# Moving first inputs, square roots and constant products across stage borders in an eleven-stage audio tower

## The reference, cut to what matters

```python
h = tokenizer(x)                       # conv1 + max over 8, conv2 + max over 4, self attention, conv3
h = h + attention0(layernorm(h))       # its own norm1, local and linear attention, then norm2 and a GELU MLP of 256
h = h + experts0(layernorm(h))         # 16 experts of 128, top 2 of a softmax gate, layernorm at the end
h = h + attention1(layernorm(h))       # 8 heads over 128 tokens, softmax
h = h + experts1(layernorm(h))         # 32 experts of 16, the best one alone, ReLU

def layernorm(x): return (x - mean(x)) / sqrt(var(x) + 1e-5)
```

## Time and profile before

| | us |
|---|---|
| median of 3 executions | 1010.16 |
| lowest and highest | 1009.18, 1010.31 |
| the profiled execution's own time | 1008.98 |
| its span, first to last instruction | 1007.1 |

### The profile page before, as it was taken

The page is one execution under the profiler, slowest core; times in us unless marked ns, Lnnn a source line. Parts: engine busy times, 40 slices in busy tenths (PEclk is TensorE's granted clock), DMA queues, the critical chain, the costliest instruction groups (busy, mean ns, idle before and its releaser), DMA issues. The chain is left out here.

```text
span 1007.1 us, 35503 instructions
## 1 busy us (share of the span) xinstructions
PE 937.3 (93%) x12674; PEld 676.7 (67%) x12674; DVE 704.2 (70%) x1964; ACT 642.4 (64%) x1204; POOL 520.2 (52%) x814
## 2 busy tenths in 40 slices
PE   7799987799889899999999997899999999969998
PEld 2345555577657688888888884566666666648887
DVE  3667744577758468787887876788888888865443
ACT  1245465687766568777777865777777777734444
POOL 0000114688675477878787876356565656452110
PEclk7799998899989899999999998999999999989999
DMA  8633000000000000000000000000000000000001
GB/s 224 146 43 59 5 2 1 2 0 0 1 2 0 3 3 4 0 0 0 0 0 0 1 2 2 1 2 1 0 0 0 0 0 0 1 2 18 21 21 28
DMA packets 10769, 14.89 MB, mean 15 GB/s; under 512 B 9296, under 2 KB 9424, under 8 KB 9680
## 3 DMA queue, kind: packets, MB, share of 16 engines
q1 hardware_dynamic: 10608, 13.63, 6.2%
q10 hardware_dynamic: 96, 0.39, 0.2%
HBM read 11.92 MB, written 2.10 MB: 14 GB/s over the span
## 5 line engine op out<-in xcount | busy, mean ns | idle before, releaser
L1771 ACT ACTIVATE e_hid<-ps,cst 128x512 f32<-128x512 f32 x256 | 155.3, 688 | 55.4 <-PE ps L1546 55.4
L1484 POOL TENSOR_TENSOR e_acc<-e_acc,e_part 128x512 f32<-128x512 f32 x96 | 122.4, 1275 | 33.7 <-DVE e_part L1702 26.8
L1558 PEld LDWEIGHTS ps<-ew,e_hid 128*64 128x64 f32 x4096 | 124.8, 138 | 22.0 <-issue 10.4
L1558 PE MATMUL ps<-ew,e_hid 128*64 128x64 f32 x4096 | 133.8, 224 | 0.0
L1546 PE MATMUL ps<-e_xs,ew 64*128 64x256 f32 x1024 | 129.8, 393 | 0.0
L1702 DVE TENSOR_TENSOR e_part<-ps,e_wt 128x512 f32<-128x512 f32 x128 | 86.8, 687 | 45.1 <-PE ps L1558 37.9
L1546 PEld LDWEIGHTS ps<-e_xs,ew 64*128 64x128 f32 x1024 | 94.9, 189 | 15.3 <-issue 3.0
L1965 POOL TENSOR_TENSOR a_sum<-a_part 128x256 f32<-128x256 f32 x64 | 46.7, 729 | 94.7 <-DVE a_part L2071 94.7
L2033 PEld LDWEIGHTS ps<-cst,a_ex 128*128 128x128 f32 x512 | 55.8, 141 | 51.5 <-issue 51.5
L2060 DVE TENSOR_REDUCE a_rmax<-ps 128x8 f32<-128x1024 f32 x64 | 78.1, 1221 | 15.9 <-PE ps L2025 14.1
L2025 PE MATMUL ps<-a_u,a_xs 64*128 64x512 f32 x256 | 71.9, 638 | 12.7 <-DVE a_diff L2063 11.6
(11 more groups left out here) (258 smaller groups left out, 2014.7 us busy)
## 6 DMA issues: line engine op xcount, KB each, us to landing
x_in<-x_dram SPq DMA_DIRECT2D x45, 128.0 KB, 5.0
cst<-cst_dram SPq DMA_DIRECT2D x1, 3101.0 KB, 13.5
out_dram<-e_res SPq DMA_DIRECT2D x16, 128.0 KB, 2.0
ew<-ew_dram SPq DMA_DIRECT2D x1, 1024.0 KB, 15.5
cst<-cst_dram SPq DMA_DIRECT2D x1, 704.0 KB, 4.5
ew<-ew_dram SPq DMA_DIRECT2D x1, 512.0 KB, 16.7
x_in<-x_dram ACTq DMA_DIRECT2D x3, 128.0 KB, 6.0
cst<-cst_dram SPq DMA_DIRECT2D x1, 153.5 KB, 4.3
```

Of the source, the lines that this page charges most:

```text
L1484: eng.tensor_tensor(acc[:, :, :, :], acc[:, :, :, :], part[n % RING][:, :, :, :], ALU.add).then_inc(sum_sb.sem, 1)
L1558: mm = eng.matmul(m.ps[rows, 6 + n % 2, to:to + C], hid[e % 8][:, a:a + C], w2[:, e * C:e * C + C], start=True, stop=True)
L1771: nc.scalar.activation(hid[e % 8][:, :].rearrange("p (r t) -> p r t", r=2), m.ps[:, 2 + 2 * (n % 2):4 + 2 * (n % 2), j * 256:(j + 1) * 256 ...
```

## The change

It moves work across stage borders and adds no arithmetic. In its parts:

1. **Start.** Each of the first six DMAs is split in two halves of 64 KB. The first halves count on a new semaphore `x_first`. `conv1` of round 0 waits for them before its first quarter, and for the second halves before its third. SP waits for the first halves alone.
2. **End of the tokenizer.** The bias products, which used bank 6, use bank 0 and stand in round 8 on PE, with their copies on DVE. `weights(2)` goes to round 8 as well, `weights(3)` to the head of round 9, before `attend`. The first turn of a0 stands before the last `conv3`. ACT copies a0's first inputs before `scaled()`, and no longer loads the Exp table there.
3. **First rounds of a0.** DVE does the late variance and inverse of n1 before round 0. The late square root stands on ACT right after the first `features`, then the Exp table is loaded once.
4. **a0 to m0.** PE turns m0's first inputs before the last `attend` and `out`; ACT copies them before `attended`; DVE does the inverse before the last `context`.
5. **m0 to e0.** The square root of n3 and a reload of the GELU table stand on ACT at the head of m0's round 15; its inverse at the end of that round on DVE. PE turns e0's first inputs before the last `out`. ACT copies them before the Exp table is loaded. The bias transposes of e0's round 0 move into the round. The hidden banks change places (4, 5 for even pairs, 2, 3 for odd).
6. **e0 to a1.** POOL makes the inputs of a1's round 1 after e0's last `fold` and `scale`. DVE does `result(14)` and `count(14)` after a1's first scores.
7. **a1 to e1.** The square root of n6 stands after sample 0 of a1's last round, its inverse after sample 1. POOL makes e1's inputs of rounds 0 and 1 after its samples 2 and 3 of that round. PE turns and ACT copies the first ones before a1's last samples, and the first routing (`logits`, then `choose` on DVE) stands among them.

```diff
-    def load_half(eng, g, b, r):
+    def load_half(eng, g, b, r, some=slice(0, H2), sem=None):
         for k in range(3):
-            rows = m.x[bass.ds(g * GS, GS), :, r * H2 + k:r * H2 + k + H2].rearrange("s c l -> (s c) l")
+            lo = r * H2 + k + some.start
+            rows = m.x[bass.ds(g * GS, GS), :, lo:lo + some.stop - some.start].rearrange("s c l -> (s c) l")
             a = 64 * r + 16 * k
-            eng.dma_start(x_in[b][a:a + 16, :], rows).then_inc(x_sem[b], 16)
-
-    m.load_first = lambda eng: load_half(eng, 0, 0, 1)
+            eng.dma_start(x_in[b][a:a + 16, some], rows).then_inc(sem or x_sem[b], 16)
+
+    def load_first(eng, r):
+
+        load_half(eng, 0, 0, r, slice(0, H2 // 2), x_first)
+        load_half(eng, 0, 0, r, slice(H2 // 2, H2))
+
+    m.load_first = lambda eng: load_first(eng, 1)
 
     def sp(eng):
 
-        load_half(eng, 0, 0, 0)
-        eng.wait_ge(x_sem[0], 96)
+        load_first(eng, 0)
+        eng.wait_ge(x_first, 96)
...
-            if h == 0:
+            if isinstance(g, int) and g == 0 and h == 0:
+                eng.wait_ge(x_first, 96)
+            elif h == (2 if isinstance(g, int) and g == 0 else 0):
                 eng.wait_ge(x_sem[b], (g - b) * 48 + 96)
...
+            last = not among(g, 0, NG)
+            tail = not among(g, 0, NG - 1) and not last
+            if last:
+                weights(3)
             if among(g, 2, NG + 1):
                 attend(g - 2, b)
             if among(g, 1, NG - 2):
                 conv1(g + 1, 1 - b, 3)
-            if not among(g, 0, NG - 1):
-                weights(2 * (g - NG))
-            if not among(g, 0, NG):
-                weights(3)
-                m.early["a0_pe"](eng)
+            if tail:
+                weights(0)
+                m.early["a0_biases"](eng)
+            if last:
+                m.early["a0_turn"](eng)
             if among(g, 2, NG + 1):
                 conv3(g - 2)
-            if not among(g, 0, NG - 1) and among(g, 0, NG):
+            if tail:
                 weights(1)
+                weights(2)
...
                 m.early["a0_scaled"](eng)
+                m.early["a0_biases_sb"](eng)
...
+                m.early["a0_act"](eng)
                 scaled()
-                m.early["a0_act"](eng)
...
-            eng.preload_act_table(ACT.Exp)
...
+    def early_turn(eng):
+        eng.wait_ge(pre_sb, 5)
         turn_inputs(eng, 0, 0)
...
+    def early_biases_sb(eng):
+        eng.wait_ge(pre, 5)
+        eng.tensor_copy(bias_kv[:, :], m.ps[:, 0, 0:1]).then_inc(pre_sb, 1)
+        eng.tensor_scalar(bias_q[:, :], m.ps[:, 0, 1:2], SCALE, None, ALU.mult).then_inc(pre_sb, 1)
+        eng.tensor_copy(bias_tok[:, :], m.ps[:, 0, P:2 * P]).then_inc(pre_sb, 1)
+        for c in range(2):
+            eng.tensor_tensor(m.m0_bias[:, c:c + 1], m.ps[:, 0, 2 + c:3 + c],
+                              m.cst[:, AT["bm1"][0] + c:AT["bm1"][0] + c + 1], ALU.add).then_inc(pre_sb, 1)
...
+            if left is None:
+                m.early["m0_turn"](eng)
...
+            if left is None:
+                m.parts["n2"][2](eng, 0)
             if back:
                 context(g - 1)
-            if left is None:
-                m.parts["n2"][2](eng, 0)
...
+        m.left["tokenizer"]()
         eng.wait_ge(pre_sb, 5)
         tokens(0, 0)
+        key_maxima(0)
         query_maxima(0, 0)
-        key_maxima(0)
-        eng.tensor_scalar(m.wm1[:, :], col(m, "wm1"), col(m, "n2g"), None, ALU.mult).then_inc(m.wm1_sem, 1)
-        m.left["tokenizer"]()
+        m.parts["n1"][2](eng, 1)
...
+                m.early["m0_act"](eng)
...
-            if left == 2 and not back:
-                m.parts["n1"][1](eng, 1)
...
+        m.parts["n1"][1](eng, 1)
+        eng.preload_act_table(ACT.Exp)
...
+            if left is None:
+                m.early["e0_turn"](eng)
             if back:
                 out(g - 1, 1 - b)
...
+            if left == 0:
+                m.parts["n3"][2](eng, 0)
...
+            if left == 0:
+                m.parts["n3"][1](eng, 0)
+                eng.preload_act_table(ACT.Gelu)
...
-            else:
-                m.early["pool"](eng, 1 - more, 1 - more)
+            elif more:
+                m.early["pool"](eng, 0, 0)
...
             scale(g - 1)
+            m.early["pool"](eng, 1, 1)
             centre(g)
...
-                    mm = eng.matmul(m.ps[:, 2 + 2 * (n % 2) + r, j * 256:(j + 1) * 256],
+                    mm = eng.matmul(m.ps[:, 4 - 2 * (n % 2) + r, j * 256:(j + 1) * 256],
...
-                if k == 0:
+                if k == 0 and not back:
+                    turn_weights(g, b)
+                if k == (0 if back else 2):
                     biases(g)
-                    if more:
-                        logits(g + 1, 1 - b)
+                if k == 0 and more:
+                    logits(g + 1, 1 - b)
...
-            result(g - 1)
-            count(g - 1)
+
+        def scaled():
+            result(TG - 2)
+            count(TG - 2)
+            normal(TG - 1)
...
-    START = (2, 4, 0, 6)
+    START = (4, 2, 0, 6)
...
-               after={"round": lambda: eng.wait_ge(T.norm[0], 4), TS: lambda: m.early["e1"](eng)})
+               after={"round": lambda: eng.wait_ge(T.norm[0], 4), ("last", 2): lambda: m.early["e1"](eng, 0),
+                      ("last", 3): lambda: m.early["e1"](eng, 1)})
...
+        after = {"tail": lambda: m.early["e1_turn"](eng), TS: lambda: m.early["e1_logits"](eng)}
...
-        after[TS] = lambda: m.parts["n6"][2](eng, 0)
+        after["last", 1] = lambda: m.parts["n6"][2](eng, 0)
+        after[TS] = lambda: m.early["e1_choose"](eng)
...
-                 "tail": lambda: m.parts["n6"][1](eng, 0)}
+                 ("last", 0): lambda: m.parts["n6"][1](eng, 0), "tail": lambda: m.early["e1_act"](eng)}
...
+    m.early["e1_turn"] = lambda eng: T.pe(eng, 0, 0)
+    m.early["e1_act"] = lambda eng: T.act(eng, 0, 0, hid_ps)
+    m.early["e1_logits"] = lambda eng: logits(eng, 0, 0)
+    m.early["e1_choose"] = lambda eng: choose(eng, 0, 0)
```

149 lines of the change are left out of this document (75 added, 74 removed).

## The result

| | before | after |
|---|---|---|
| median, us | 1009.67 | 985.35 |
| lowest to highest of 4 | 1008.77 to 1010.31 | 982.16 to 985.77 |
| span of the profiled execution | 1007.1 | 980.4 |
| mean granted clock in it | 0.962 | 0.977 |

The ratio is 0.9769 with a 95% interval of 0.9745 to 0.9792, so the kernel after is 24.3 us faster by the medians. The forecast was 20.7 us less, 989.5 us, with a range of 981 to 998. The result lies in it, but nearer to the 983.5 us of the rival "the clock stays up" than to 989.5. The profiled execution took 982.16 us and is the fastest of the four. The other three took 985.3 to 985.8 us, so the trace flatters the change by some 3 us. A second set of five executions of the same kernel, beside the last experiments, had a median of 986.56 us (before there: 1008.97, ratio 0.9793, interval 0.9771 to 0.9815). That is 22.4 us.

A forecast was written before the change was run, and what follows sets the result against it. PE was taken as the bound mid-stage, with time to gain from its idle time and its spells at 1.2 GHz. -2.5 -9.7 -0.5 +0 -3.7 -4.3 = -20.7 us, from 1010.2 to 989.5 us, range 981 to 998.

The forecast's parts named there:

- the clock stays up: Rival: with idle times gone at four borders, the stretches at 1.2 GHz go too; 983.5 us, chance 0.17.
- Start: Tokenizer's start: halved first inputs make the first round ready sooner, limited by the DMA queue; -2.5 us, bounds -3.6 and -1.
- the DMA stream: Limit at the start: weights and round 2's input keep the queue full, and it starts only some 2 us sooner.
- Parts 2 and 3: Tokenizer's end and a0's first rounds: 3.9 us from reordered products, 5.8 from the early root; -9.7 us, bounds -4.5 and -11.4.
- half of a0's gain only: Rival: keys and exponentials trail three more rounds in a0, giving 1 instead of 5.8 us; 994.3 us, chance 0.15.
- Part 4: Border a0 to m0: first hidden product about 0.5 us sooner, table loads stay; -0.5 us, bounds +0.5 and -1.5.
- Part 5: Border m0 to e0: earlier inverse and turn, but `out` then stands before the gate's products; 0 us, bounds -1.5 and +1.5.
- Part 6: Border e0 to a1: DVE's last sum 2.8 us sooner, second score 3.9 sooner; -3.7 us, bounds -2 and -5.
- Part 7: Border a1 to e1: routing moves among a1's last samples, at 0.9 us cost there; -4.3 us, bounds -2 and -6.
- Slower: Rival: e0's 16 rounds each lengthen through bank meetings or later biases; 1015 us at 1.6 us a round, chance 0.03.
- dear switches: Rival: ACT falls behind in m0's round 15 and a1's last round by twice the count; 994.5 us, chance 0.08.
- bank conflict: In e0's middle: new banks could make PE and ACT meet in one bank, lengthening rounds; slower from 1.3 us a round.

The follow-up runs named there:

- u1: The kernel after with only the halved first inputs undone, so they come in six whole DMAs: 991.13 us, ratio 0.9833.
- b: The kernel before with six warm products without use in place of four, inputs unchanged: 1004.89 us, ratio 0.9976.
- u3: The kernel after with only the early square root of n1 undone, back at the end of a0's round 0: 993.06 us, ratio 0.9863.
- u2: The kernel after with the tokenizer's bias and last weights products and a0's first turn put back behind attend: 992.89 us, ratio 0.9847.
- after_again: The kernel after, unchanged, executed once more beside later experiments on the same chip: 986.56 us, ratio 0.9793.
- v8: The kernel after with GpSimd's inputs of a1's round 1 moved ahead of e0's last centre and scale, the bias add last: 984.07 us, ratio 0.9756.
- v6: The kernel after with GpSimd's product for a1's round 1 and the bias moved behind e0's last centre: 985.37 us, ratio 0.979.

## Why the prediction was right, and where it wasn't

**Start: -2.5, right within what can be told.** A is 55.67 us before and 50.08 to 53.27 in the eleven traces with halves, their median 52.46, so some 3 us; against u1's 54.53 it is 2. The medians of the executions put 4.6 to 5.8 us on it, and what lies between stays open. The step had two errors. I took the `conv1` at 33.95 for round 2's. It is the last quarter of round 1; round 2's is at 36.50. And I let the stream start "some 2 us sooner". SP was released 3.3 us sooner (9.38 to 6.04), because it now waits for half of the data. The limit that I named, the DMA stream, shows in five traces, with waits of 1.33 to 4.01 us; in seven of ten traces of this start it doesn't, and there PE is idle in A for 9.38 us instead of 10.69. The idle time that I expected before the third quarter isn't there either. So the number fits in part by luck. I also put nothing on the clock, and priced each quarter at 1.78 us for both kernels. The 16 products took 3.70 us in u1 and b, so that price was the clock's.

**Parts 2 and 3: -9.7.** By undoing them one by one, 4.1 and 4.9, together 9.0 against my 3.9 and 5.8. B and C together were 142.82 before and are 131.9 in most traces after, so 10.9. Of the 1.9 us more, 1.2 are idle time in C that only the kernel before has (9.70 us, against 8.49 in u3), and 0.7 is the higher clock that u2 met in C. The steps held: the wait before `attend` is gone, the last `conv3` takes 2.1 us, one table load takes the place of two, and round 1's `features` comes 5.9 us after the first (I had 6.7). The rival "half of a0's gain only" is out.

**Part 4: -0.5, measured -0.9. Part 5: 0, measured -0.4** in idle time of its stretch; what its executions say (3 us) is open. In the first trace they looked like -2.9 and -2.1. The rival "the clock stays up" claimed such gains at 0.17. It is half true: the clock is higher after (27.6 or 22.5 us lost instead of 38.3), but not at these borders in every execution. Of the 22.3 us between the traces of before and after_again, 14.5 are idle time: 1.3 in A, 1.4 in B, 5.1 in C, 0.1 in D, 0.4 in E, 2.2 in G, -0.9 in H and 4.8 in I. The other 7.8 are PE's busy time. My sum had some 2.6 of those (3.06 us of products priced at 1.9, and `conv3` at 2.1 instead of 3.49), and nothing at the other borders. So by this count the waits gave some 3.6 us less than the 18.1 I had for them, and the clock some 5.2 more. The two misses offset each other, and that the sum came so near is luck to that extent.

**Part 6: -3.7, measured -2.2. This is the step that failed**, though the sum stayed in its range, as other parts brought more than forecast. I had GpSimd's work for a1 go "behind `fold` and `scale`" and took VectorE's small operations there at their old lengths. They now run beside GpSimd's product and addition, and two of them take 1.04 and 0.60 us instead of 0.17 and 0.16. These 1.3 us are most of the 1.5 that are missing, and v8 gives them back. The Trainium skill ("SBUF — State Buffer", section "SBUF: two separate sides") names such a case: an operation of VectorE with two inputs in SBUF and one of GpSimd that reads SBUF exclude each other for the whole instruction, and whoever starts first keeps the other out. The rows of v6 and v8 agree, the statistics with their one input included. I had not set this rule against the new order.

**Part 7: -4.3, measured -4.6 to -6.1.** The cost of 0.9 us in the last round was about right (mostly 0.8 to 1.6 in H). The routing came 0.9 us sooner than worked out: from a1's last score to the second routing it took 12.38 us, where my times give 13.3. In idle time the part is worth 3.9; what is above that is the clock.

**Slower, and dear switches.** The bank conflict did not show at any size that matters: F is longer by 0.4 us in all, in sixteen rounds. What these 0.4 us are is open. A table load is followed by its function after 0.02 us in the rows above. By the Trainium skill ("ScalarE: Activation LUTs", section "What ACT_TABLE_LOAD costs") each switch would have cost 1.38 us more. The trace disagrees: 0.02 us behind the load leave no room for it, and the measurement decides.

## What to carry to other kernels

Undo one part at a time and compare the same stretch in all traces: 3 us at one border were the clock's choice, while other stretches repeated to 0.02 us. Split each stretch into busy and idle time of PE: the idle time repeated where the length did not, and showed the 0.4 us of part 5. When work is moved to another engine's idle time, look at what the neighbouring engine does in that time, since even an operation of 0.17 us can stand for the length of the other's. And look at what a wait releases: with whole inputs the DMA queue was let go 3.1 us later, and round 2 then waited 4.01 us for its data.

## What the runs showed of the hardware

A two-input operation of VectorE on SBUF took 1.04 us instead of 0.17 when it began together with a 128x512 product on GpSimd, and 0.28 when it began 0.26 us before that product's end. Another took 0.60 instead of 0.16 beside an addition on GpSimd. Both were back at 0.17 and 0.16 with the product moved away. Beside the same product BATCH_NORM_STATS2 kept its 0.60 us. PE's first 16 `conv1` products took 3.70 us at 2.4 GHz (granted clock 1.00) after an idle 1.13 us in one kernel, and 7.10 us at 1.2 GHz (0.52 over the products) after an idle 2.07 us in another.
